# Context attention of a two-layer decoder: score maxima taken from four PSUM places of 512 columns, probabilities weighed two chunks late, the shift turned in halves, and the first maxima over 128 rows

## The reference

```python
x        # 1 x 1024 x 128, the output of the Mamba block and its norm
ctx      # 1 x 6404 x 128
q = (x @ w_q) split into 16 heads of 8
k, v = split(ctx @ w_kv, 2)             # one key head and one value head of 8, shared by all 16 heads
p = softmax(q @ k.T / sqrt(8))          # per head: 1024 x 6404
out = concat(p @ v) @ w_concat
```

## Time and profile before

| | us |
|---|---|
| runs of the kernel (3): median | 2249.99 |
| lowest, highest | 2240.22, 2252.94 |
| the profiled execution's own time | 2255.29 |
| its span, first to last instruction | 2253.6 |
| TensorE, VectorE, ScalarE busy in the span | 2100.2, 1590.2, 1319.3 |
| GpSimd busy | 120.0 |
| mean granted TensorE clock (1 is 2.4 GHz) | 0.952 |

### The profile page before, as it was taken

How to read it: one execution, slowest core, us unless ns; L and a number is a source line. 1 busy time by engine, 2 the same in 40 slices (tenths; PEclk the granted TensorE clock), 3 DMA queues, 4 the chain that set the end, 5 groups by cost and what they waited for, 6 DMA issues and landing times. The chain is left out here.

```text
span 2253.6 us, 38636 instructions
## 1 busy us (share of the span) xinstructions
PE 2100.2 (93%) x15240; PEld 995.6 (44%) x15240; DVE 1590.2 (71%) x2158; ACT 1319.3 (59%) x2189; POOL 120.0 (5%) x156
## 2 busy tenths in 40 slices
PE   8777999999999999999999999899589997999898
PEld 5223343333333333333333333477533333777755
DVE  4997578898888988889888882223778873444335
ACT  4232157777777777777777778533247773333421
POOL 1560000000000000000000000000200010000000
PEclk7898599999999999999999999899779999999989
DMA  4110000000000000000000000011000000000011
GB/s 135 56 65 0 0 1 1 1 1 1 1 1 1 1 1 1 1 1 1 1 1 1 1 1 1 13 33 35 1 1 1 0 0 0 1 1 0 1 33 33
DMA packets 22978, 24.59 MB, mean 11 GB/s; under 512 B 5728, under 2 KB 20224, under 8 KB 22576
## 3 DMA queue, kind: packets, MB, share of 16 engines
q1 hardware_dynamic: 21648, 20.44, 3.0%
q10 hardware_dynamic: 1184, 2.10, 0.2%
HBM read 21.81 MB, written 0.59 MB: 10 GB/s over the span
## 5 line engine op out<-in xcount | busy, mean ns | idle before, releaser
L959 DVE TENSOR_REDUCE sb_max_partial<-ps_max_ps 128x1 f32<-128x1024 f32 (+1 forms) x896 | 958.1, 1107 | 110.1 <-PE ps_max_ps L802 104.4
L950 ACT ACTIVATE sb_probs<-ps_score_ps 128x512 f32<-128x512 f32 (+1 forms) x1632 | 885.3, 595 | 237.9 <-PE ps_score_ps L922 195.2
L802 PE MATMUL ps_max_ps<-sb_key_stack,sb_q_stack 64*128 64x512 f32 (+1 forms) x1664 | 608.5, 443 | 21.7 <-DVE sb_max_partial L959 9.1
L922 PE MATMUL ps_score_ps<-sb_q_stack,sb_key_stack 64*128 64x512 f32 x1632 | 592.5, 442 | 1.9 <-issue 0.4
L903 PE MATMUL ps_acc_ps<-sb_probs,sb_val_ones 128*32 128x256 f32 x6528 | 521.4, 391 | 0.9 <-ACT sb_probs L950 0.4
L922 PEld LDWEIGHTS ps_score_ps<-sb_q_stack,sb_key_stack 64*128 64x128 f32 x1632 | 241.0, 185 | 281.1 <-ACT sb_probs L950 266.3
L802 PEld LDWEIGHTS ps_max_ps<-sb_key_stack,sb_q_stack 64*128 64x128 f32 x1664 | 256.9, 188 | 159.1 <-DVE sb_max_partial L959 135.3
L903 PEld LDWEIGHTS ps_acc_ps<-sb_probs,sb_val_ones 128*32 128x32 f32 x6528 | 128.4, 108 | 293.0 <-ACT sb_probs L950 218.6
L1654 DVE TENSOR_REDUCE sb_s_max_partial<-ps_s_max_ps 128x1 f32<-128x512 f32 x256 | 170.2, 690 | 42.5 <-PE ps_s_max_ps L1579 35.7
L1644 ACT ACTIVATE sb_s_probs<-ps_s_score_ps 128x1024 f32<-128x1024 f32 x128 | 131.0, 1024 | 49.0 <-PE ps_s_score_ps L1616 46.6
L1871 DVE TENSOR_SCALAR_CACHE_REDUCE sb_x_scores<-ps_x_score_ps 128x1024 f32<-128x1024 f32 (+1 forms) x56 | 62.1, 1111 | 80.7 <-PE ps_x_score_ps L1812 80.7
(11 more groups left out here) (279 smaller groups left out, 1738.7 us busy)
## 6 DMA issues: line engine op xcount, KB each, us to landing
sb_val<-c_rows SPq DMA_DIRECT2D x16, 512.0 KB, 3.7
sb_e_w<-L_ffn_rW SPq DMA_DIRECT2D x30, 128.0 KB, 2.0
sb_e_w<-L_ffn_W_T SPq DMA_DIRECT2D x24, 128.0 KB, 2.1
sb_ctx_T<-ctx_T SPq DMA_DIRECT2D x1, 1664.0 KB, 7.8
sb_ctx_T<-ctx_T ACTq DMA_DIRECT2D x1, 1538.0 KB, 8.7
sb_x_T<-x_T SPq DMA_DIRECT2D x1, 512.0 KB, 4.0
sb_x_tok<-x ACTq DMA_DIRECT2D x1, 512.0 KB, 11.0
sb_e_w<-L_ffn_sW SPq DMA_DIRECT2D x4, 128.0 KB, 3.7
```

The source lines that it names most:

```text
L802: ins = nc.tensor.matmul(max_ps[:, u % 2, a:a + n], q_stack[rows(blk), blk // 2, h * P:(h + 1) * P], k.key_stack[rows(blk), c0 + a:c0 + a ...
L922: nc.tensor.matmul(score_ps[:, e % 3, :], k.key_stack[rows(blk), c * P:(c + 1) * P], q_stack[rows(blk), blk // 2, j * HALF:(j + 1) * HALF] ...
L950: nc.scalar.activation(probs[0:n, c % 3, j * HALF:(j + 1) * HALF], score_ps[0:n, e % 3, :], ACT.Exp).then_inc(exp_done, 1)
L959: nc.vector.tensor_reduce(partial[:, h, r:r + 1], max_ps[:, u % 2, 0:RANGES[r][1]], AX.X, ALU.max).then_inc(unit_used, 1)
```

## The change

- **Places.** `max_ps` becomes four places of 512 columns. A tile is now one matmul of at most 512 columns, 13 to a head, 104 to a block, and VectorE reduces each alone. What uses a place is fixed by a list (`order`); an item waits until the item four before it is used.
- **Order.** The loop puts one tile after each score matmul (101 tiles over the 96 half chunks up to chunk 47, so five times two), and `weigh` of chunk c-2 between the two score matmuls instead of `weigh` of chunk c-1 after both.
- **Shift.** The negated maxima are made and turned in halves of four heads. Half A is turned at chunk 28 and copied by ScalarE, half B at the end of chunk 50, among the first three tiles of the block after next, and copied by VectorE. Each score matmul of a new block's first chunk waits for its own half only.
- **First maxima.** `q_first` is block 0's query stack with rows 64 to 127 zero, copied by GpSimd; block 0's tiles use all 128 rows. The low part of the queries is now made by a TensorE matmul that subtracts the high part (`minus_low`), and ScalarE copies it; VectorE no longer takes part in making queries.
- **Values.** `values` and `take_values` leave the Mamba block. Five new jobs (`val0_jobs`, 51 chunks of matmuls with 8 moving columns) run during the first maxima, and ScalarE copies them.

```diff
-                keys.values(pe, w_kv, range(0, 12))
...
-                keys.values(pe, w_kv, range(12, NCH))
...
-                pe.wait_ge(keys.v_taken, 1)
...
-                keys.take_values(dve)
...
-            max_ps = k.ps("max_ps", [P, 2, WIDE], tmp)
+            max_ps = k.ps("max_ps", [P, PLACES, HALF], tmp)
...
+            TURN_AT, LAST_AT, FIRST_TURN = 28, 48, 66
+            FEW = 3
...
+            def border(b):
+                return [(b + 1, 0), (b, "B"), (b + 1, 1), (b + 1, 2)] if b + 1 < NB else [(b, "B")]
...
+                        for j in range(2):
+                            n = (count * (2 * c + j + 1)) // (2 * LAST_AT) - (count * (2 * c + j)) // (2 * LAST_AT)
+                            now[j].extend((b + 1, u) for u in todo[:n])
+                            del todo[:n]
+                        if c == TURN_AT:
+                            now[1].append((b + 1, "A"))
...
+            def free_place(pe, item):
+
+                if place[item] < PLACES:
                     return
...
+            def max_tile(pe, blk, u):
+                h, (c0, n) = u // NR, RANGES[u % NR]
+                if blk == 0:
+                    queries, keys = q_first[:, h * P:(h + 1) * P], k.key_stack[:, c0:c0 + n]
...
+            def subtract_high(pe, i):
+
+                pe.wait_ge(q_high, i + 1)
+                nc.tensor.matmul(q_bank(i), k.minus_low[:], q_rows(i), start=False, stop=True,
+                                 skip_group_check=True).then_inc(q_minus, 1)
...
-                pe.wait_ge(q_ready, blk + 1)
...
+                        if c == 0:
+                            pe.wait_ge(shift_ready["AB"[j]], blk + 1)
...
-                    if with_max and c <= LAST:
-                        max_unit(pe, blk + 1, u)
-                        u += 1
-                    if c >= 1:
-                        weigh(pe, blk, c - 1)
...
-                    if with_max and c == NCH - 2:
-                        turn_shift(pe, blk + 1)
+                        for item in items_at[blk * NCH + c][j]:
+                            issue(pe, item)
+                        if j == 0 and c >= LAG:
+                            weigh(pe, blk, c - LAG)
...
                     for blk in range(NB):
-                        attend(pe, blk, blk < NB - 1)
-                    weigh(pe, NB - 1, NCH - 1)
+                        attend(pe, blk)
+                    for v in range(NCH - LAG, NCH):
+                        weigh(pe, NB - 1, v)
```

339 lines of the change are left out of this document (194 added, 145 removed).

## The result

The changed kernel takes 2143.43 us (median of 4 runs, 2139.72 to 2146.2) against 2245.1 us (4 runs, 2237.77 to 2252.94): a ratio of 0.9546, 95% interval 0.9504 to 0.9587, 102 us less. The forecast was 2167 and the range 2142 to 2206, so the direction came out as forecast, and the time 1.4 us inside the fast end of the range (one of the four runs lies outside it). What has to be explained is a gain of 102 us where 83 were summed up.

A forecast was written before the change was run, and what follows sets the result against it. A block was taken to be TensorE's time, with VectorE 5 to 10 us behind. Terms -14.8, -58 and -10 sum to -83 against the profiled 2255.3, giving 2172, or a median of 2167 us; range 2142 to 2206.

The forecast's parts named there:

- The nearest single forecast, 2153: Rival: clock stays high in the first maxima (-17) and VectorE hides wholly (block of 66.4, -65); chance 0.12.
- Values out of the Mamba block: Mamba block: without the late value matmuls and copies, the scan-opening step starts at about 39.25 instead of 54.04, -14.8 us.
- Blocks: Blocks 0 to 14: 66.9 us a block, 3.9 less, together -58 us; block 15 unchanged.
- I take 0.34: First maxima: each of 104 max matmuls over 128 rows priced at 0.34 us, 34.4 in all; bounds 0.22 and 0.34.
- The sum for the kernel before: A block before: chunks 63.2, nine extra units 6.1, turned shift 0.96, wait for its copy 0.57; sum 70.8 us.
- VectorE hides: Inside a block: VectorE needs 63.3 of 66.9 us, reductions 0.61 each, so TensorE covers it, thinly.
- the rival (2198): VectorE becomes the bound: stalls on places delay scores, a block takes 69 us, gain 27 instead of 58; chance 0.20.
- First maxima: Stretch before block 0: 96 us at full clock plus 7 for low clock, 103 us, -10; bounds -17 and +15.
- The rival in which it holds for 64 us: Clock stays low in the first maxima: +15 us there instead of -10, kernel at 2192; chance 0.15.
- No drain that costs anything that way: Inside a block, from 64-row score to 128-row weighing: 0.33 us against 0.34 score to score, so the change costs nothing.
- Pairs break: Rival: tiles start after their scores instead of beside them, 0.34 us each; with half unpaired, 2432 us; chance 0.06.
- blocks don't gain: Rival: savings in unpaired tiles return as waits for places; only Mamba and first maxima count, 2225 us; chance 0.07.

The follow-up runs named there:

- first experiment: Layer 0's values made in the Mamba block again, the five value jobs removed, against the changed kernel: 2139.83 us, ratio 0.9529.
- second experiment: Block 0's tiles read 64 rows of the query and key stacks instead of 128, against the changed kernel: 2166.11 us, ratio 0.9652.

## Why the prediction held, and which terms were mis-sized

**The total.** That 2143 still lies in the range from 2142 on is in part luck: the two terms that missed erred the same way, and 1.5 us more would have left the range. The nearest single forecast, 2153, had the clock stay high in the first maxima, which it did not.

**Values out of the Mamba block.** -14.8 forecast, -15.2 in the trace, the step that opens the scan at 39.8 for a forecast 39.3. That the two agree so well is luck: with the values put back the stretch grows by 10.3 only (first experiment). And as a price of the edit it is half of the account, since 11.6 us of matmuls moved behind it and the clock fell there: with both ends counted the edit is worth nothing. The prediction had both terms, but booked the second under the first maxima, where other gains hid it.

**Blocks.** 66.9 forecast, 66.06 measured, 3.9 and 4.7 less than before. The base of 51 chunks was 63.2, and is 63.0. The term that was mis-sized is the tile without a partner: 5 x 0.34 = 1.7 forecast, 4 x 0.23 = 0.9 measured, since the fifth and last finds a partner, the first score of chunk 48, which has no tile of its own. Border, turns and ScalarE's copy were 0.7 + 1.1 + 0.2 = 2.0, and are 2.3 (0.63 and 0.10 at half A, 0.84, 0.56 and 0.15 at the border). The 0.7 for two of the four tiles at the border is right by accident: three have no partner, because of their rows, at 0.23 each. Together 66.2, a tenth more than measured. "I take 0.34" came from reading 1.19 us for four matmuls as four equal shares. The first of a row stands 0.34 ahead of the second, the others are 0.23 apart (in the trace of before they start at 229.43, 229.77, 230.00 and 230.23): 0.34 is the first matmul behind a change of kind, whose weight load starts together with it.

The sum for the kernel before was also right by accident. It came to the measured 70.8, but by the starts of its scores the nine extra units cost 6.6 us above the plain pace, not 6.1, because waits for a place are in it, and the wait for the shift 0.15 and not 0.57. What paid for the gain follows from that. The surplus of tiles went from 6.6 to 0.9 us a block; turns, border and the rest went the other way, from 1.2 to 2.3. Of the edits, the lag gave 0.15 us a block and the halves -0.13. The rest of the 4.7 is, by subtraction, the smaller tile in four places, of which one and not two is surplus at a time and none waits for a place; no run parts the size of the tile from the number of places. With three places of 512 it would be 3.3, with two a loss of 8.

ScalarE's copy of the sums is the term that the prediction had at 0.2, and it is the 0.09 of chunk 3:

```profile
799.03 0.37 ACT L984 COPY sb_gathered<-ps_acc_ps 128x256 f32<-128x256 f32 x1 [0.29 <-PE ps_acc_ps L959]
799.30 2.07 ACT L994 ACTIVATE sb_probs<-ps_score_ps 128x512 f32<-128x512 f32 x4
```

The exps of chunk 1 start only behind the copy, the second of them ends at about 800.40, and the weights of chunk 3's first score, which needs its bank, load at 800.45 instead of 0.11 behind the load before, at 800.25.

**VectorE hides.** Right, and better than feared: the rival (2198) is excluded by the measured block, 66.06 for its 69, and by the run that took 37% of VectorE's time away for 0.04 us a block. Reductions in a row are about 0.60 apart (7 in 4.27, the last of 0.68), for 0.61 forecast.

**First maxima.** -10 forecast, -23.0 measured, the largest miss. Their mechanism was right (more TensorE work, less of VectorE's, some low clock), the sizes were not. Working back from 90.4 us with 24 us at the low level (178.3 to 181.6 and 202.0 to 222.5), full clock would give 78.5 instead of the forecast's 96. Tiles took 0.23 instead of 0.34: 11.4 us for 104; the 16 subtractions likewise: 1.8; the first tile came 5.2 us into the stretch instead of 7.5: 2.3. These make 15.5 of the 17.5. An fp32 matmul of 512 columns takes 0.86 (two times 0.43) between 128-row neighbours, not 0.95: another 2.6 for 28.5 of them, so that the terms overshoot by about 0.6. The lower bound of 0.22 was the right end; "since it is the same data type" chose the wrong one. The low clock cost 12 us instead of 7, in 24 us instead of 15 (by the run with the values spread, 10 of them in the 20.5).

**The clock.** "It fell while 64-row tiles stood between 128-row jobs" made the rows of the tile look like the cause. The tiles on 64 rows add 14 us of low clock in one trace, so they may have a part in it, but in the changed kernel the fall comes with value jobs of up to 13 chunks in a row and vanishes when they are spread. That does not explain the kernel before, which has no such job there and is low for 64 us: 64-row tiles without value jobs were not run in the changed kernel, so their part stays open. The rival in which it holds for 64 us fell; so did the one in which it never falls, for the kernel as changed. The rule of the Trainium skill (TensorE: Matmul & The Clock Gate, Why this matters for your kernels) that keeping TensorE continuously busy brings full rate is not borne out here: from 202.0 to 222.5, as the profile counts busy time, it is busy 20.50 of 20.50 us at 0.50, which is 1.2 GHz.

**"No drain that costs anything that way."** Wrong. The 0.33 us from score to weighing was compared with 0.34 from score to score, and both hold 0.1 us of a change of kind. Plain pace is 0.23. Since the kernel has as many such changes per chunk as before, the sum did not suffer; it did in the first maxima, where 128-row tiles take them away: about 15 us by the second experiment, part of the same 0.34 that stood for a tile.

**Pairs break, blocks don't gain.** Score and tile start within 0.01 us of each other; neither rival came.

What stays open: why the value jobs in a row bring the clock down and fewer at a time do not, and what brought it down in the kernel before.

## What to carry to other kernels

Take the price of one more matmul in a row from the distance between the second and the third start, never from a row's length divided by its count: the first carries a weight load and a change of rows that the others don't. When a cheap piece of work is moved off one stretch, price it again where it lands, with what stands beside it there. Before a piece of work is counted as free beside another, look which rows each uses: a tile of the block after next sits on the rows of the scores around it and pairs with none. And when two engines run level through a shared buffer, one place too few costs far more than the average load says: here 79.0, 67.5 and 66.06 us for two, three and four.

## What the hardware showed that I had not expected

- Changing between matmuls over 128 rows and over 64 rows costs up to 0.19 us a change, 0.09 in front and 0.10 behind; over 97 changes it came to 15 us, 0.15 each.
- Fp32r matmuls of 512 columns follow each other in 0.23 us, over 64 rows as over 128.
- The granted clock fell to 0.50 with TensorE busy without a gap, in a stretch of matmuls with 8 moving columns, and stayed there for 20.5 us; with the same matmuls spread in fours it stayed at 1.00. Ahead of the first maxima it fell at 174.7 behind an idle TensorE in the changed kernel, and at 173.8 with TensorE busy with such matmuls in the version with 20 chunks there.
- Matmuls on different halves of the rows do not start in the order of the program: the score at 796.15 stands behind two tiles in the program and starts before the second of them (796.48). So the sentence above that instructions of one engine go in program order does not hold for the starts of such matmuls.
